# Probabilities turned one slot behind their scores in the front slots, and idle products in the first slots and at the fp8 rows

## The chip, the cores and the metric

The kernel runs on one core of a Trainium2 chip. The metric is the device time of one execution in microseconds. Five engines work side by side and meet only at semaphores: TensorE (PE in the profile, with its weight loads as PEld), VectorE (DVE), ScalarE (ACT), GpSimd (POOL) and SyncE (SP), whose queue issues the DMAs.

## What is computed

The reference is a stack of four pairs of cross-attention and feed-forward on x of 32 sequences x 64 rows x 128 columns, with a context of the same shape. The residual stream x runs through all of them:

```python
x = x + _L0_xattn_ref(_layernorm(x), ctx, mask, ...)   # 16 heads of width 64
x = x + _L0_ffn_ref(_layernorm(x), ...)                # six layers of local attention and a gated MLP
x = x + _L1_xattn_ref(_layernorm(x), ctx, ctx, ...)    # 16 heads of width 8
x = x + _L1_ffn_ref(_layernorm(x), ...)                # rows quantised to fp8, one product
x = x + _L2_xattn_ref(...); x = x + _L2_ffn_ref(...)   # experts, top 2 of 8, and a shared one
x = x + _L3_xattn_ref(...); x = x + _L3_ffn_ref(...)   # experts, top 2 of 8
```

The change lies in the small cross-attentions L1 and L2 (`n` = 0, 1 in the code), as far as they run ahead of the experts. For a tile of 128 rows (two sequences) one of them is: normalise x, project queries, keys and values, scores of 16 heads (128 x 1024 logits), subtract the maximum, exp, product with the values, divide by the sum, output projection, add to x.

## The kernel before, in words

x lies in SBUF as 16 tiles of 128 rows. `layers_*` run L0 (some 1600 us), then `merged_*` run the rest as a row of *slots* u = 0, 1, 2, ... A slot holds up to one piece of each of three *works* in flight. A work W is one small cross-attention of one tile; in the front slots, u < `LEAD` = 16, work W starts in slot W. In the program, `work` is the one that starts (u), `before` the one of the slot before (u - 1), `before2` the one before that (u - 2). From slot 16 on each slot also carries an expert; those slots are untouched. The order on each engine is written out by hand, and there is no scheduler.

What a work does, with the lines of the kernel before:

- in slot W: TensorE turns the normalised x (`turn_x`, L1676), ScalarE copies it (L1880), TensorE makes keys (L1723), values (L1732) and queries (L1739); ScalarE adds biases and copies (`front`, L1893 and L1895), VectorE spreads the keys over eight groups of heads (`keys`, L2016);
- in slot W + 1: scores (L1704) into a bank of PSUM, two of which are used: `w0` for odd W from 3 to 11, `w1` for the rest; VectorE takes maxima and subtracts them (`shift`, L1998, L2000), ScalarE makes the exp (L1901), TensorE turns the probabilities back into the same bank (eight transposes, L1750), ScalarE copies them to `probT` (L1907);
- in slot W + 2: product with the values (`attend`, L1687), VectorE divides by the sums (L2007, L2010), TensorE turns the rows (L1714), ScalarE adds a bias (L1886), TensorE makes the output product (`rows`, L1744), VectorE adds it to x (L2023) and takes statistics (L476, L478), from which GpSimd makes a scale and a shift in four small steps;
- in slot W + 3: ScalarE normalises the new x with them (`fresh_normalise`, L1912).

The output product L1744 also waits until VectorE has spread the keys of the slot's own work. The scores of a work wait until the bank's previous probabilities are copied. In slots 7 and 11 (`PRODUCT_AT`) the fp8 rows come in: VectorE quantises four tiles at the end of the slot before (L2124 to L2133, 5.2 us), TensorE turns them (L1795), ScalarE copies them (L1917), TensorE multiplies (L1803), ScalarE copies (L1978), VectorE adds (L2139). `occupy` (L1761) is a product of the identity with a weight into a bank that nobody reads (an idle product); it does no part of the computation. In slots 0 to 3 the last pieces of L0 run too (`layers_in_slot`): slot 1 has three hidden chunks of its MLP (L841, L847) and their output product (L853); VectorE's gate L1209 stands between.

Of the kernel before, what the change touches and what calls it, by code (L numbers as in the profile page):

```python
# [18 lines left out]
PAIRS = HEADS // 2  # L19
# [547 lines left out]
def layers_tensor(pe, k):  # L567
# [264 lines left out]
    def end_hidden(Q, c):  # L832
        at, n = CHUNKS[c]
        xnT = quad_buffers(k, Q).xnT
        if c:
            pe.wait_ge(k.gated, 3 * Q + c)
        else:
            pe.wait_ge(k.xn_ready, Q + 1)
            if Q < LAST:
                pe.wait_ge(k.qT_ready, FIRST + STEPS)  # L840
        pe.matmul(k.end.gates[0:n, :], k.c_w1[:, HID + at:HID + at + n], xnT[:, :], start=True,  # L841
                  stop=True).then_inc(k.gate_psum, 1)
        if c:
            pe.wait_ge(k.hid_ready, 3 * Q + c)
        elif Q == LAST:
            pe.wait_ge(k.z_fed, LAST)
        pe.matmul(k.end.lines[0:n, :], k.c_w1[:, at:at + n], xnT[:, :], start=True, stop=True).then_inc(k.line_psum, 1)  # L847

    def end_output(Q):
        pe.wait_ge(k.hid_ready, 3 * Q + 3)  # L850
        for c in range(3):
            n = CHUNKS[c][1] + (c == 2)
            mm = pe.matmul(k.end.lines, k.c_w2[0:n, c, :], quad_buffers(k, Q).hid[0:n, c, :], start=(c == 0), stop=(c == 2))  # L853
        mm.then_inc(k.out_psum, 1)

    def end_of_layers():
# [12 lines left out]
        end_hidden(LAST - 1, 2)  # L869
        end_in()  # L870

    def in_slot(u, place):

        if (u, place) == (0, "end"):
            end_output(LAST - 1)
            turn_out(1)
        if (u, place) == (1, "scores"):
            end_turn()
        if (u, place) == (1, "end"):
            for c in range(3):  # L880
                end_hidden(LAST, c)
            end_output(LAST)
        if (u, place) == (2, "end"):
            turn_out(2)
        if (u, place) == (3, "end"):
            turn_out(3)
# [4 lines left out]
    for g in range(-TILES, STEPS + 1):  # L891
        this, before, before2 = stages_of(g)
# [584 lines left out]
LEAD = 16  # L1477
END_SLOTS = 2
# [91 lines left out]
def on_w0(W):  # L1570

    return W % 2 == 1 and END_SLOTS < W < LEAD - 3
# [16 lines left out]
def merged_tensor(pe, k, layers_in_slot):  # L1589
    d = k.d  # L1590
# [78 lines left out]
    def turn_x(W, u):  # L1669
        pe.wait_ge(k.norm.normed, PHANTOM + W + TILES + 1)  # L1670
        pe.wait_ge(d.q_ready, started(u))
        pe.wait_ge(d.v_ready, started(u))
        pe.wait_ge(d.oT_ready, started(u - 2))
        if u == 0:
            pe.wait_ge(k.xn_ready, LAST)
        pe.transpose(k.pt[:, 0:P], k.normed[:, W % 2, :], k.ident[:, :]).then_inc(d.xT_psum, 1)  # L1676
# [66 lines left out]
        pe.wait_ge(d.k8_ready, started(u + 1))  # L1743
        pe.matmul(k.py[:, P:2 * P], k.s_oT[:, :], k.s_w[:, n, 3, :], start=True, stop=True).then_inc(d.y_psum, 1)  # L1744

    def turn_pairs(W, pairs):
        w = logits_bank(k, W)
        pe.wait_ge(d.exp, PHANTOM + W + 1)
        for h in pairs:
            mm = pe.transpose(w[:, h * P:(h + 1) * P],  # L1750
                              k.prob[:, W % 2, 2 * h:2 * h + 2, :].rearrange("p a m -> p (a m)"), k.ident[:, :])
        return mm

    def turn_probs(W):
        turn_pairs(W, range(PAIRS)).then_inc(d.pT_psum, 1)

    def occupy():

# [5 lines left out]
    def front_slot(u, work, before, before2):  # L1764
        if work:
            turn_x(work[2], u)
        if before:
            scores(before[2])
        layers_in_slot(u, "scores")
        if work:  # L1770
            keys(*work, u)
        if before2:
            attend(before2[2], u)
        if work:
            values(work[0], work[2], u)
            queries(work[0], work[2])
        if u in PRODUCT_AT:
            turn_quantised(PRODUCT_AT[u])
        layers_in_slot(u, "end")
        if u > END_SLOTS:  # L1780
            occupy()
        if before2:
            turn_rows(before2[2], u)
        if before:
            turn_pairs(before[2], range(PAIRS // 2))
        if before2:
            rows(before2[0], before2[2], u)
        if before:
            turn_pairs(before[2], range(PAIRS // 2, PAIRS)).then_inc(d.pT_psum, 1)

    def turn_quantised(q):
        pe.wait_ge(k.f.quantised, q + 1)
# [70 lines left out]
def merged_scalar(act, k, layers_in_slot):  # L1863
    d = k.d
# [64 lines left out]
    for u in range(SLOTS):  # L1929
        work, before, before2 = work_at(u), work_at(u - 1), work_at(u - 2)  # L1930
        job = job_at(u)
        if job:
            gelu(job, 0)
        if work:
            turned_x(work[2])
        if work_at(u - 3):
            fresh_normalise(*work_at(u - 3)[1:])
        if job:
            gelu(job, 1)
        if u in PRODUCT_AT and u >= LEAD:  # L1940
            turned_quantised(PRODUCT_AT[u])
        if job:
            gelu(job, 2)
        if before2 and u >= LEAD:
            turned_rows(before2[0], before2[2], u)
        if job:
            gelu(job, 3)
        layers_in_slot(u, "turned x")
        if work:
            front(work[0], work[2])  # L1950
        layers_in_slot(u, "front")
        if u < LEAD:
            if u in PRODUCT_AT:
                turned_quantised(PRODUCT_AT[u])
            if before:
                exp(before[0], before[2])
            if before2:
                turned_rows(before2[0], before2[2], u)
            if before:
                turned_probs(before[2])  # L1960
        if u in GATES_TURN_AT:
            e, q = GATES_TURN_AT[u]
            act.copy(k.m_gateT[0:NE[e], 512 * q:512 * q + 512], full(("gates", e, q))[0:NE[e], :]).then_inc(k.ring_read, 1)
        if u in TURN_AT:
            e, q = TURN_AT[u]
            act.copy(k.m_xT[:, q, :], full(("turn", e, q))).then_inc(k.ring_read, 1)
        if u in GATES_AT:
            quad_exp(*GATES_AT[u])
        if before and u >= LEAD:
            exp(before[0], before[2])  # L1970
        if (before and u >= LEAD) or u in GATES_AT or u == LEAD - 1:
            gelu_table(u)
        if before and u >= LEAD:
            turned_probs(before[2])
        if u in PRODUCT_AT:
            q = PRODUCT_AT[u]
            act.wait_ge(k.f.done, q)
            act.copy(k.f_prod, full(("product", q))).then_inc(k.ring_read, 1)  # L1978
        if u in RAW_AT:
            w = full(("raw", 1, RAW_AT[u]))  # L1980
            act.copy(k.m_projT[:, :], w)
            act.activation(k.m_sq[:, :], w, ACT.Square).then_inc(k.ring_read, 1)
        if u in LOGITS_AT:
            e, q = LOGITS_AT[u]
            n = 36 if e else 32
            act.copy(k.m_raw[:, 0:n], full(("logits", e, q))[:, 0:n]).then_inc(k.ring_read, 1)
        if u == SIM_AT:
            act.copy(k.m_simT[:, :], full(("sim", 1, 0))[:, 0:8]).then_inc(k.ring_read, 1)
# [491 lines left out]
```

## Time and profile before

| | us |
|---|---|
| median of 3 timed runs | 2417.6 (2416.79 to 2418.31) |
| the profiled execution, its own time | 2425.08 |
| span of its trace | 2423.3 |
| TensorE busy | 2342.5 (97%) |
| VectorE busy | 1870.4 (77%) |
| ScalarE busy | 1505.6 (62%) |
| GpSimd busy | 1216.4 (50%) |
| mean granted clock of TensorE | 0.987 |

The front slots take the stretch from 1610 to 1758 us of the trace. The engines' shares are averages over the whole program, so what the change does has to be read in that stretch alone: which wait ends last in a slot, how long a slot is, and which clock TensorE was granted there (1.00 is 2.4 GHz, 0.50 is 1.2 GHz).

### The profile page before, as it was taken

To read this page: it belongs to the slowest core of one execution; us is meant where nothing else is said; L and a number is where in the kernel's file an instruction comes from. 1 tells how busy PE (TensorE), PEld (TensorE's weight loads), DVE (VectorE), ACT (ScalarE), POOL (GpSimd) and SP (SyncE) were. 2 spreads that over 40 slices of the span, in tenths; PEclk is the share of its full clock that TensorE was granted. 3 is DMA by queue.
4 is the path that set the end of the run, shared out by engine and by line. 5 is a ranking of instruction groups with operands and counts; after the bars stand their busy time and mean duration, and the time that the engine had idled before them with its cause. 6 is when DMAs were issued, how large, how long until landed. Compare 5 with 4: busy or idle time off the path is not lost.

```text
span 2423.3 us, 61019 instructions
## 1 busy us (share of the span) xinstructions
PE 2342.5 (97%) x25478; PEld 1422.6 (59%) x25478; DVE 1870.4 (77%) x3328; ACT 1505.6 (62%) x2190; POOL 1216.4 (50%) x1028
## 2 busy tenths in 40 slices
PE   8998999999999999999999999987899999999998
PEld 6785566666666666666666666655445555455443
DVE  6989989999999999999999989957756765445222
ACT  3444666666666666666666666654477777566443
POOL 2336777777777777777777777722211121111000
PEclk9999999999999999999999999998899999999999
DMA  3000000000000000000000100002010110120110
GB/s 129 9 7 6 2 2 28 11 8 7 28 11 8 7 28 11 13 2 28 10 13 3 35 2 11 2 4 89 9 38 9 41 33 15 55 86 29 38 41 22
DMA packets 36183, 56.30 MB, mean 23 GB/s; under 512 B 6396, under 2 KB 20868, under 8 KB 35656
## 3 DMA queue, kind: packets, MB, share of 16 engines
q1 hardware_dynamic: 35912, 52.40, 6.8%
q8 instruction: 205, 3.36, 0.6%
q14 instruction: 66, 0.54, 0.1%
HBM read 51.19 MB, written 1.19 MB: 22 GB/s over the span
## 4 chain that ended last, share of the span: by engine, by line
PE 73%; DVE 19%; ACT 4%; issue 3%; POOL 1%; DVEq 0%; ACTq 0%; POOLq 0%
PE w L1621 9%; PE w L1611 9%; PE w L679 6%; PE w L660 6%; PE w L670 5%; DVE turned L1161 4%; PE w L430 4%; PE py L700 4%; PE w L724 3%; PE w L753 3%; PE w L734 2%; DVE norm L1168 2%; PE pt L783 2%; PE py L787 2%; PE w L1750 2%
## 5 line engine op out<-in xcount | busy, mean ns | idle before, releaser
L441 ACT ACTIVATE prob<-logit 128x512 f32<-128x512 f32 x224 | 137.9, 632 | 285.0 <-DVE logit L449 285.0
L1611 PE MATMUL w<-qT,m_fc 128*128 128x512 f32 x544 | 267.8, 605 | 0.4 <-ACT turned L1875 0.4
L1346 POOL TENSOR_TENSOR straight_odd<-straight_odd,turned 128x1024 f32<-128x1024 f32 x96 | 226.6, 2371 | 65.6 <-DVE turned L1161 65.6
L471 POOL TENSOR_TENSOR prob<-prob,rden 128x1024 f32<-128x1024 f32 x112 | 213.9, 1909 | 91.0 <-DVE rden L460 91.0
L1161 DVE TENSOR_TENSOR turned<-w,rot 128x512 f32<-128x512 f32 x384 | 245.5, 681 | 0.0
L1346 POOL TENSOR_TENSOR straight<-straight,turned 128x1024 f32<-128x1024 f32 x96 | 226.7, 2372 | 36.1 <-DVE turned L1161 36.1
L1340 POOL TENSOR_TENSOR straight_odd<-straight_odd,rnorms 128x1024 f32<-128x1024 f32 x96 | 180.7, 1903 | 118.2 <-DVE rnorms L1182 118.2
L1168 DVE TENSOR_REDUCE norm<-sq 128x16 f32<-128x1024 f32 x192 | 224.2, 1209 | 0.0
L490 POOL TENSOR_TENSOR fresh_roots<-fresh_means,eps 128x1 f32<-128x1 f32 x64 | 12.3, 191 | 386.1 <-DVE fresh_means L478 386.1
L1340 POOL TENSOR_TENSOR straight<-straight,rnorms 128x1024 f32<-128x1024 f32 x96 | 180.7, 1903 | 42.9 <-DVE rnorms L1182 42.9
L679 PE MATMUL w<-b_wqkv,m_proj 128*128 128x512 f32 x384 | 190.4, 618 | 1.9 <-DVE logit L449 1.9
L660 PE MATMUL w<-b_wqkv,m_proj 128*128 128x512 f32 x384 | 190.4, 618 | 0.0
L670 PE MATMUL w<-b_wqkv,m_proj 128*64 128x512 f32 x768 | 186.0, 605 | 3.3 <-DVE oT L1141 3.3
L700 PE MATMUL py<-oT,b_wo 128*128 128x256 f32 x768 | 181.5, 379 | 0.0
L2060 DVE SCALAR_TENSOR_TENSOR gate<-w,m_bcol,b_wqkv 128x512 f32<-128x512 f32 x60 | 45.0, 751 | 160.6 <-PE w L1621 160.4
L700 PEld LDWEIGHTS py<-oT,b_wo 128*128 128x128 f32 x768 | 142.2, 190 | 38.2 <-issue 23.3
L1875 ACT ACTIVATE turned<-w,m_bfc 128x512 f32<-128x512 f32 x136 | 93.4, 688 | 104.0 <-PE w L1611 102.3
L1875 ACT ACTIVATE straight_odd<-w,m_bfc 128x512 f32<-128x512 f32 x136 | 93.6, 689 | 99.9 <-PE w L1611 98.3
L1068 ACT COPY qT<-w 128x1024 f32<-128x1024 f32 x96 | 97.4, 1015 | 93.0 <-PE w L712 91.4
L457 DVE TENSOR_REDUCE den<-prob 128x8 f32<-128x512 f32 x224 | 143.5, 682 | 10.1
L1611 PEld LDWEIGHTS w<-qT,m_fc 128*128 128x128 f32 x544 | 92.1, 191 | 97.7 <-issue 88.8
L430 PEld LDWEIGHTS w<-probT,v 64*64 64x64 f32 x7168 | 115.1, 135 | 56.0 <-issue 52.3
(290 smaller groups left out, 5353.3 us busy)
## 6 DMA issues: line engine op xcount, KB each, us to landing
b_wqkv<-gates SPq DMA_DIRECT2D x64, 256.0 KB, 3.6
b_wqkv<-in_b_wqkv SPq DMA_DIRECT2D x18, 512.0 KB, 3.5
ctxT<-in_ctxT SPq DMA_DIRECT2D x64, 64.0 KB, 1.8
b_wo<-in_b_wo SPq DMA_DIRECT2D x6, 512.0 KB, 4.0
m_fc<-in_m_fc SPq DMA_DIRECT2D x1, 2304.0 KB, 8.5
m_proj<-in_m_proj SPq DMA_DIRECT2D x1, 2304.0 KB, 13.1
m_fc<-in_m_fc SPq DMA_DIRECT2D x8, 256.0 KB, 3.4
m_proj<-in_m_proj SPq DMA_DIRECT2D x8, 256.0 KB, 3.4
```

The source lines that it names most:

```text
L430: mm = pe.matmul(w[64 * c:64 * c + 64, at:at + 64], k.v2[r, s, b, 64 * h:64 * h + 64], k.probT[r, h, 64 * b:64 * b + 64], start=True, stop ...
L471: pool.tensor_tensor(flat, flat, k.rden[:, s, :, None].broadcast_to([P, HEADS, SEQ]), ALU.mult).then_inc(k.prob_ready, 1)
L660: mm = pe.matmul(k.w0[:, 512 * c:512 * c + 512], shifted_rows(k, g % TILES), k.b_wqkv[:, 512 * c:512 * c + 512], start=True, stop=True)
L670: mm = pe.matmul(k.w2[64 * p:64 * p + 64, 512 * b:512 * b + 512], k.z[:, 2 * t + b, :], k.b_wqkv[:, 2048 + 512 * p:2560 + 512 * p], start= ...
L679: mm = pe.matmul(k.w1[:, 512 * c:512 * c + 512], shifted_rows(k, g % TILES), k.b_wqkv[:, 1024 + 512 * c:1536 + 512 * c], start=True, stop= ...
L700: mm = pe.matmul(k.py[:, 0:2 * P], k.b_wo[:, h, :], k.oT[:, h, :, :].rearrange("p a n -> p (a n)"), start=(h == 0), stop=(h == PAIRS - 1))
L1161: last = dve.tensor_tensor(k.turned[:, i, :, to], heads[:, :, of], rot[:, 2 * i + 1, None, to].broadcast_to([P, HEADS, half]), ALU.mult)
L1168: dve.tensor_reduce(k.norm2[:, i, :], k.sq[:, i, :, :], AX.X, ALU.add).then_inc(norm2, 1)
L1340: pool.tensor_tensor(k.straights[s][:, i, :, :], k.straights[s][:, i, :, :], k.rnorms[:, s, i, :, None].broadcast_to([P, HEADS, HD]), ALU. ...
L1346: pool.tensor_tensor(k.straights[s][:, i, :, :], k.straights[s][:, i, :, :], k.turned[:, i, :, :], ALU.add).then_inc(added, 1)
L1611: pe.matmul(claim(("hidden", J, c)), k.m_fc[:, x, c * P:(c + 1) * P], k.m_xT[:, q, :], start=True, stop=True).then_inc(k.ring_full, 1)
L1621: mm = pe.matmul(acc, k.m_proj[:, x, c, :], k.m_hid[J % 2][:, c, :], start=(c == 0), stop=(c == 3))
```

## The change

In the front slots TensorE turns the probabilities of a work in the slot after its scores' slot: `turn_probs(before2)` instead of `turn_pairs(before)`. Where the two works use one bank (`together`: slots 2, 3, 14 and 15) it stands before the scores, elsewhere behind them. `attend` moves behind the queries. In slot 15 the last probabilities are turned at the slot's end as well, since slot 16 is as it was. On ScalarE the copy `turned_probs` moves from the slot's end to a place behind `fresh_normalise` and ahead of `front`, and the exp moves behind `turned_rows`. Idle products are added: one behind each hidden chunk in slot 1 (`layers_idle`), two before and two behind the turned fp8 rows in slots 7 and 11, and one in slot 2. VectorE's, GpSimd's and SyncE's instructions keep their order.

```diff
--- before.py
+++ after.py
@@ -869,6 +869,10 @@
         end_hidden(LAST - 1, 2)
         end_in()
 
+    def layers_idle():
+
+        pe.matmul(k.end.turn, k.ident[:, :], k.s_w[:, 0, :, :].rearrange("p a n -> p (a n)"), start=True, stop=True)
+
     def in_slot(u, place):
 
         if (u, place) == (0, "end"):
@@ -879,6 +883,7 @@
         if (u, place) == (1, "end"):
             for c in range(3):
                 end_hidden(LAST, c)
+                layers_idle()
             end_output(LAST)
         if (u, place) == (2, "end"):
             turn_out(2)
@@ -1743,16 +1748,13 @@
         pe.wait_ge(d.k8_ready, started(u + 1))
         pe.matmul(k.py[:, P:2 * P], k.s_oT[:, :], k.s_w[:, n, 3, :], start=True, stop=True).then_inc(d.y_psum, 1)
 
-    def turn_pairs(W, pairs):
+    def turn_probs(W):
         w = logits_bank(k, W)
         pe.wait_ge(d.exp, PHANTOM + W + 1)
-        for h in pairs:
+        for h in range(PAIRS):
             mm = pe.transpose(w[:, h * P:(h + 1) * P],
                               k.prob[:, W % 2, 2 * h:2 * h + 2, :].rearrange("p a m -> p (a m)"), k.ident[:, :])
-        return mm
-
-    def turn_probs(W):
-        turn_pairs(W, range(PAIRS)).then_inc(d.pT_psum, 1)
+        mm.then_inc(d.pT_psum, 1)
 
     def occupy():
 
@@ -1764,29 +1766,35 @@
     def front_slot(u, work, before, before2):
         if work:
             turn_x(work[2], u)
+        together = before and before2 and on_w0(before[2]) == on_w0(before2[2])
+        if together:
+            turn_probs(before2[2])
         if before:
             scores(before[2])
         layers_in_slot(u, "scores")
+        if before2 and not together:
+            turn_probs(before2[2])
         if work:
             keys(*work, u)
+            values(work[0], work[2], u)
+            queries(work[0], work[2])
         if before2:
             attend(before2[2], u)
-        if work:
-            values(work[0], work[2], u)
-            queries(work[0], work[2])
         if u in PRODUCT_AT:
+            occupy()
+            occupy()
             turn_quantised(PRODUCT_AT[u])
+            occupy()
+            occupy()
         layers_in_slot(u, "end")
-        if u > END_SLOTS:
+        if u >= END_SLOTS:
             occupy()
         if before2:
             turn_rows(before2[2], u)
-        if before:
-            turn_pairs(before[2], range(PAIRS // 2))
         if before2:
             rows(before2[0], before2[2], u)
-        if before:
-            turn_pairs(before[2], range(PAIRS // 2, PAIRS)).then_inc(d.pT_psum, 1)
+        if before and u == LEAD - 1:
+            turn_probs(before[2])
 
     def turn_quantised(q):
         pe.wait_ge(k.f.quantised, q + 1)
@@ -1946,17 +1954,19 @@
         if job:
             gelu(job, 3)
         layers_in_slot(u, "turned x")
+        if before2 and u < LEAD:
+            turned_probs(before2[2])
         if work:
             front(work[0], work[2])
         layers_in_slot(u, "front")
         if u < LEAD:
             if u in PRODUCT_AT:
                 turned_quantised(PRODUCT_AT[u])
-            if before:
-                exp(before[0], before[2])
             if before2:
                 turned_rows(before2[0], before2[2], u)
             if before:
+                exp(before[0], before[2])
+            if before and u == LEAD - 1:
                 turned_probs(before[2])
         if u in GATES_TURN_AT:
             e, q = GATES_TURN_AT[u]
```

TensorE, one front slot that holds nothing special (slot 5), before. The names: `normed` is the normalised tile, `straight` and `s_qT` keys and queries, `ctxT` the context, `s_v` the values, `s_rows` the divided rows, `s_oT` the turned rows.

```order
L1676 MATMUL pt<-ident,normed 128x128
L1704 MATMUL w1<-straight,s_qT 64x512 x4
L1723 MATMUL py<-ctxT,s_w 128x128
L1687 MATMUL w2<-s_v,probT 64x18 x16
L1732 MATMUL pt<-s_w,ctxT 64x64 x4
L1739 MATMUL pt<-xT,s_w 128x128
L1761 MATMUL w2<-s_w,ident 128x512
L1714 MATMUL w2<-ident,s_rows 128x128
L1750 MATMUL w1<-ident,prob 128x128 x4
L1744 MATMUL py<-s_w,s_oT 128x128
L1750 MATMUL w1<-ident,prob 128x128 x4
```

The same slot now:

```order
L1681 MATMUL pt<-ident,normed 128x128
L1709 MATMUL w1<-straight,s_qT 64x512 x4
L1755 MATMUL w0<-ident,prob 128x128 x8
L1728 MATMUL py<-ctxT,s_w 128x128
L1737 MATMUL pt<-s_w,ctxT 64x64 x4
L1744 MATMUL pt<-xT,s_w 128x128
L1692 MATMUL w2<-s_v,probT 64x18 x16
L1763 MATMUL w2<-s_w,ident 128x512
L1719 MATMUL w2<-ident,s_rows 128x128
L1749 MATMUL py<-s_w,s_oT 128x128
```

The transposes went from both sides of the output product to behind the scores, in the other bank, and belong to the work before; the attend that reads their copy went from behind the keys to behind the queries.

ScalarE, a slot of the same kind, before:

```order
L1880 COPY xT<-pt 128x128
L1912 ACTIVATE y_all<-x_all,fresh_below,fresh_roots 128x128
L1893 ACTIVATE s_qT<-pt,s_cols 128x128
L1895 COPY s_v<-pt 64x16x8 x2
L1901 ACTIVATE prob<-logit 128x1024
L1886 ACTIVATE s_oT<-w2,s_cols 128x128
L1907 COPY probT<-w1 128x1024
```

and now:

```order
L1888 COPY xT<-pt 128x128
L1920 ACTIVATE y_all<-x_all,fresh_below,fresh_roots 128x128
L1915 COPY probT<-w0 128x1024
L1901 ACTIVATE s_qT<-pt,s_cols 128x128
L1903 COPY s_v<-pt 64x16x8 x2
L1894 ACTIVATE s_oT<-w2,s_cols 128x128
L1909 ACTIVATE prob<-logit 128x1024
```

The copy of the probabilities went from the end of the row to behind the fresh normalisation, whose input is GpSimd's, and the exp to the end.

TensorE in slot 15, now, with what follows it (before, the slot reads like slot 5 before):

```order
L1681 MATMUL pt<-ident,normed 128x128
L1755 MATMUL w1<-ident,prob 128x128 x8
L1709 MATMUL w1<-straight,s_qT 64x512 x4
L1728 MATMUL py<-ctxT,s_w 128x128
L1737 MATMUL pt<-s_w,ctxT 64x64 x4
L1744 MATMUL pt<-xT,s_w 128x128
L1692 MATMUL w2<-s_v,probT 64x18 x16
L1763 MATMUL w2<-s_w,ident 128x512
L1719 MATMUL w2<-ident,s_rows 128x128
L1749 MATMUL py<-s_w,s_oT 128x128
L1755 MATMUL w1<-ident,prob 128x128 x8
L1640 MATMUL w2<-ident,y_all 128x128 x4
```

Here both rows of transposes and the scores are in bank `w1`: the transposes stand first, and a second set closes the slot.

## Rows read from the trace of the kernel before

**Rows 1.** The page, busy time of each engine, share of the span, instructions.
```profile
PE 2342.5 (97%) x25478; PEld 1422.6 (59%) x25478; DVE 1870.4 (77%) x3328; ACT 1505.6 (62%) x2190; POOL 1216.4 (50%) x1028
```

**Rows 2.** Stretches of slots 3, 4, 5+6, 7+8, 9+10, 11+12, 13, 14+15: length, busy, clock.
```profile
1640.97:1652.92 11.95, 10.97 (x76) 7.16 (x75) 6.15 (x13) 3.90 (x8) 2.24 (x7) 0.50 0.02 7
1652.92:1660.85 7.93, 5.99 (x69) 3.74 (x68) 6.17 (x13) 3.90 (x8) 2.23 (x7) 1.00 0.29 82
1660.85:1674.18 13.33, 11.74 (x135) 7.29 (x133) 10.97 (x22) 7.79 (x16) 4.46 (x14) 1.00 0.83 331
1674.18:1695.70 21.52, 15.67 (x143) 9.80 (x140) 17.19 (x36) 8.78 (x18) 5.26 (x14) 0.80 0.03 7
1695.70:1709.83 14.13, 12.55 (x134) 7.75 (x134) 10.97 (x22) 7.80 (x16) 4.46 (x14) 0.94 0.04 11
1709.83:1731.02 21.19, 14.99 (x142) 9.16 (x141) 17.19 (x36) 8.79 (x18) 5.26 (x14) 0.84 0.03 8
1731.02:1740.84 9.82, 9.76 (x68) 6.06 (x66) 5.49 (x11) 3.90 (x8) 2.23 (x7) 0.52 0.02 7
1740.84:1756.87 16.03, 12.33 (x134) 7.71 (x134) 10.97 (x22) 7.79 (x16) 4.46 (x14) 0.97 0.03 9
```

**Rows 3.** TensorE in time, slot 5: start, length, instruction.
```profile
1660.40 0.45 PE L1744 MATMUL py<-s_w,s_oT 128*128 128x128 f32 x2
...
1661.33 1.09 PE L1704 MATMUL w<-straight,s_qT 64*64 64x512 f32 x8
...
1662.77 1.11 PE L1687 MATMUL w<-s_v,probT 128*64 128x18 f32 x32
...
1664.42 1.02 PE L1761 MATMUL w<-s_w,ident 128*128 128x512 f32 x2
...
1667.06 0.46 PE L1744 MATMUL py<-s_w,s_oT 128*128 128x128 f32 x2
```

**Rows 4.** VectorE in time, slot 5: start, length, [idle before, what ended it].
```profile
1660.89 0.29 DVE L2023 TENSOR_TENSOR x_all<-x_all,py 128x128 f32<-128x128 f32 x1 [0.64 <-PE py L1744]
...
1662.48 1.23 DVE L1998 TENSOR_REDUCE top<-w 128x16 f32<-128x1024 f32 x1 [0.23 <-PE w L1704]
...
1665.43 0.29 DVE L2010 TENSOR_TENSOR s_rows<-w,rden 128x128 f32<-128x128 f32 x1
1665.64 1.28 DVE L2016 SCALAR_TENSOR_TENSOR straight<-py,s_cols,member 128x1024 f32<-128x1024 f32 x1
```

**Rows 5.** ScalarE in time, slot 5, and one row of slot 7.
```profile
1661.33 1.01 ACT L1907 COPY probT<-w 128x1024 f32<-128x1024 f32 x1 [1.07 <-PE w L1750]
...
1663.33 0.49 ACT L1912 ACTIVATE y_all<-x_all,fresh_below,fresh_roots 128x128 f32<-128x128 f32 x1 [0.82 <-POOL fresh_below L2201]
...
1677.38 0.49 ACT L1912 ACTIVATE y_all<-x_all,fresh_below,fresh_roots 128x128 f32<-128x128 f32 x1 [1.54 <-POOL fresh_below L2201]
```

**Rows 6.** TensorE in time, single rows of slots 7, 8, 13 and 14.
```profile
1679.55 0.40 PE L1795 MATMUL w<-ident,xnT 128*128 128x128 bf16 x4 [1.62 <-DVE xnT L2131]
...
1687.31 1.09 PE L1704 MATMUL w<-straight,s_qT 64*64 64x512 f32 x8
...
1731.51 1.99 PE L1704 MATMUL w<-straight,s_qT 64*64 64x512 f32 x8
...
1742.88 1.09 PE L1704 MATMUL w<-straight,s_qT 64*64 64x512 f32 x8 [1.04 <-ACT probT L1907]
```

**Rows 7.** One stretch of slot 7, columns as in rows 2.
```profile
1684.02:1687.10 3.08, 3.08 (x15) 2.66 (x16) 1.90 (x4) 0.79 (x3) 0.00 (x0) 0.51 0.00 0
```

**Rows 8.** VectorE in time, slots 7 and 8.
```profile
1683.39 0.25 DVE L2007 RECIPROCAL rden<-w 128x16 f32<-128x16 f32 x1
1683.68 0.29 DVE L2010 TENSOR_TENSOR s_rows<-w,rden 128x128 f32<-128x128 f32 x1
...
1688.50 1.36 DVE L2139 SCALAR_TENSOR_TENSOR x_all<-xs,f_scale,x_all 128x128 f32<-128x128 f32 x4 [1.49 <-ACT xs L1978]
```

**Rows 9.** TensorE in time, slot 1, the output product of the MLP.
```profile
1628.54 2.85 PE L853 MATMUL w<-v,c_w 128*128 128x512 f32 x6 [0.84 <-DVE v L1209]
```

The columns of rows 2 and 7: start:end, length, then busy time (and instructions) of PE, PEld, DVE, ACT and POOL, the granted clock of TensorE, the DMA share, GB/s.

## The prediction

> **What bounds the kernel now.** I read the engines' busy shares first: TensorE 2342.5 us of a span of 2423.3, so on the page it is the bound [rows 1]. But the change touches only the 16 front slots, about 150 us, and there the share hides the shape. Next I cut the trace at the end of each slot's output product (line 1744), which gives slot lengths and the granted clock [rows 2]: slots 5 and 6 take 13.33 us together at full clock, slots 3 and 13 take 11.95 and 9.82 at about half of it (1.2 GHz), slots 7+8 and 11+12 take 21.52 and 21.19. Then one steady slot, engine by engine, from the end of the product of slot 4 (t = 0, at 1660.40 + 0.45 = 1660.85) to the end of the next (1667.52): 6.67 us. On TensorE 1.02 us of it is an idle product [rows 3] and 0.8 us are gaps (11.74 busy of 13.33 for two slots) [rows 2]. VectorE [rows 4] adds the output at 0.04, takes the maxima at 1.63, has the scaled rows ready at 1665.72 (4.87), then spreads the keys (line 2016, 1.28 us). The product that ends the slot starts at 1667.06, 0.14 behind the end of the key spreading at 1666.92, and ends at 1667.52. So a slot ends 1.8 us after the scaled rows, call that moment S: a row ready later moves the slot's end one for one. ScalarE [rows 5] copies the turned probabilities at 1661.33, and does the fresh normalisation of an older tile at 1663.33, since that waits for GpSimd: 2.48 after t = 0, always. Today that wait holds up nobody: the copy stands ahead of it.
>
> **The change, part by part.**
>
> *Probabilities one slot later.* Per slot 8 transposes stay 8, and the exp, the copy and the output's bias are the same instructions. What moves is who waits. In the changed order ScalarE does: copy of the turned x, fresh normalisation, copy of the probabilities, biases. The copy now stands behind the wait for GpSimd. Steady slot, from rows: fresh normalisation 2.48 to 2.97, copy of 1.01 us [rows 5] overlapping its end slightly, 2.88 to 3.89, TensorE's attend at 3.95 (0.06 later, as transposes follow the exp), 1.11 us long [rows 3], to 5.06. VectorE's reciprocal and scaling after it: 5.11 to 5.68 = S (0.58 us for the two) [rows 8]. The maxima chain alone would give S at 4.7, so the attend is the later one. Slot length S + 1.8 = 7.48 against 6.67: **0.81 us longer**. TensorE fits: turned x, scores, 8 transposes, keys, values, queries take it to 3.3, where it waits 0.65 us for the copy. The exp follows the bias at once and ends about 0.1 into the next slot, before its transposes at 1.1: no cost.
>
> *Slots 3, 14 and 15*, in which the probabilities and the next scores use one bank. The transposes come first, then the scores must wait for the copy: 3.95 to 5.04. VectorE needs 3.24 us from the start of the maxima (5.09) to S (1662.48 to 1665.72) [rows 4], so S = 8.33 and the slot is 10.1 us. Today the scores there wait 1.04 us [rows 6] and the two slots 14+15 take 16.03 together. So +4.2 for both at full clock. In slot 3 TensorE also turns an output; 10.25 against 11.95: -1.7.
>
> In these slots TensorE is idle from about 1.2 to 3.95. The trace shows what such stretches bring: after the waits around 1730 the clock went to 1.2 GHz, and slot 13 ran at 0.52 [rows 2], with 1.99 us for the scores instead of 1.09 [rows 3, 6]. Estimated from the lengths of [rows 3] at up to twice: the scores take 2.0, the next three products 2, the attend 1.9, the idle product 1.7, the turned rows, bias and output 1.5: the slot ends at 12.8 instead of 10.1, and 13.5 in slot 3. That is +9.6 for slots 14+15, and +1.55 for slot 3. Both ends stay for the range.
>
> On this stands one sentence of the Trainium skill (TensorE: Matmul & The Clock Gate, Part 4: PE-mode transpose): the transpose mode doesn't count as PE-busy the same way. The trace speaks against it here: the 3.08 us from 1684.02 hold 15 TensorE instructions, 9 of them fp32 transposes, at 1.2 GHz, and right behind them the scores take 1.09 us, the length of the 2.4 GHz level [rows 6, 7]. By the rule the slots 3, 14 and 15, which put eight transposes ahead of the gap, would all run low, the upper end of what follows; by the row only part of them.
>
> *The end of slot 15.* The last probabilities are turned after slot 15's output; their copy precedes the copy that the first gate logits wait for. Exp to 0.1, transposes 0.15 to 1.2, copies to 3.2, where today they are half done before the output. From row differences: +1.1, or +1.7 at the low clock.
>
> *Slots 7 and 11 (fp8 rows).* VectorE's quantising keeps S where it is, 9.8 us after the slot's start (1683.68 + 0.29 against the start at 1674.18) [rows 2, 8]. Four more idle products of 0.86 us and the moved attend lie in TensorE's queue: attend to 5.7 (beside the quantising GpSimd is slower: fresh normalisation at 1677.38, 3.2 after the start [rows 5], so the copy ends at 4.6), two idle products to 7.4, the turned fp8 rows, which could have gone at 5.4 [rows 6], to 7.8, the copy to 8.4, three idle products to 11.0. The turned rows then leave at 11.0 instead of 9.9, and the slot ends at 12.3 against 11.9: these products are not free, +0.35 each. What they buy is the clock behind them: slots 8 and 12, with VectorE's product added at 1.2 instead of 2.4 after the start (1688.50 less 1686.08 [rows 8]; no copy of probabilities ahead of it), reach S = 6.3 and end at 8.1, against 9.6 and 9.3 today. So 7+8: 20.35 against 21.52, -1.2; 11+12: 20.35 against 21.19, -0.8. If the clock falls at the attend's 1.4 us wait, each idle product costs 1.7 us and the slot 4 us more: kept for the range.
>
> *Slot 1, idle products between the hidden chunks.* TensorE's one wait of note there is the 0.84 us before the output product [rows 9]; between the chunks it hardly waits. So two of the three products push, at 0.8 and 0.65 us each, and the third lies in the wait: +1.3 on the output product. Slot 2 gives it back, since the exp and half of the transposes no longer stand before its output: +0.1 at its end, and a full clock into slot 3 instead of 0.50.
>
> *The rest.* Slot 4 waits for VectorE's add before its scores, then the copy: 8.25 against 7.93, +0.3. Slots 5+6: +1.6. Slots 9+10: 14.96 against 14.13, +0.8. Slot 13: 7.48 against 9.82, -2.3, if the clock stays up.
>
> **Sum**, full clock everywhere: 0.1 - 1.7 + 0.3 + 1.6 - 1.2 + 0.8 - 0.8 - 2.3 + 4.2 + 1.1 = **+2.1**. With the low clock in slots 3, 14 and 15: 0.1 + 1.55 + 0.3 + 1.6 - 1.2 + 0.8 - 0.8 - 2.3 + 9.6 + 1.7 = **+11.3**. Idle stretches of 1.3 to 2.3 us on both sides of short work were enough to drop it at slots 3, 8, 12 and 13 today, and here the stretch is 2.75; it drops somewhere in the slot and not at its start, so I take two thirds of the difference: +8.2. The sums are made within the profiled execution (span 2423.3, its own time 2425.1); the median of the timed runs is 2417.6, and a difference inside 150 us is carried over unchanged: 2425.8.
>
> **Rivals.**
> A, the forecast: the copy behind GpSimd's wait sets the slots, low clock in much of slots 3, 14, 15. 2425.8, from 2422.5 to 2429. Chance 0.45.
> B: the same wait, but the clock holds: 2419.7. For it: slots 14 and 15 today hold 0.97 through waits of 1.04, 0.3 and 0.5 us. Against: one gap of 2.75. Chance 0.22.
> C, the other side: the fresh normalisation gets its input early and the copy is not late. This decides at 2.15 after the output's end, when the transposes finish; GpSimd's answer would have to come 0.3 us sooner. Then attend ends at 4.3, S stays at 4.7, steady slots are 6.5, slots 14 and 15 8.4, slot 3 8.6, slot 13 6.5. Sum: -3.4 - 0.5 - 0.4 - 1.6 - 1.2 - 1.3 - 3.3 + 0.8 + 1.1 = -9.8: 2407.8. Against: 2.48 in every slot read. Chance 0.12.
> D: the clock falls too in a slot with fp8 rows or behind it (+4): 2430 to 2434. Chance 0.13.
> E: the change doesn't do what it says: slots stay at VectorE's pace, the idle products only shift the low stretches about; 2416 to 2420. Chance 0.08.
>
> **How the numbers follow.** 2425.8 is A's. The range from 2413.5 to 2434 takes in A, B, D, E and half the way to C; it leaves out C and a little of D. A measurement here tells 0.2% (4.8 us) from no change: faster is C, 0.12; same is B, E and the lowest part of A, 0.33; slower is the rest of A and D, 0.55.
>
> **What would show it.** Right: in the changed profile the copy of the probabilities starts directly behind the fresh normalisation in slots 4 to 13; TensorE waits for it ahead of the attend, about 0.65 us; steady slots of 7.4 to 7.5; scores of slots 14 and 15 waiting over 2 us, then at 1.2 GHz; slot 13 at full clock. Wrong: steady slots of 6.5 to 6.7, or an attend that waits for nothing (C); scores of 1.09 us behind the long gap (B); a fp8 slot over 14 us (D).

## The result, and the profile after

| | before | changed |
|---|---|---|
| median, us | 2417.19 (2416.20 to 2418.31, 4 runs) | 2438.41 (2435.10 to 2439.75, 4 runs) |
| ratio | | 1.0083, 95% interval 1.0070 to 1.0096 (the two medians alone: 1.0088) |
| span of the trace | 2423.3 | 2435.7 |

The change makes the kernel 21.2 us slower. The direction was forecast, the size was not: 2425.8 with a range to 2434. The two traces differ by only 12.4 us, and the first experiment is about that.

The changed kernel, the same stretches as in [rows 2] (slots 3, 4, 5+6, 7+8, 9+10, 11+12, 13, 14+15; start:end, length, busy time and instructions of PE, PEld, DVE, ACT, POOL, granted clock, DMA share, GB/s):

```profile
1639.77:1651.13 11.36, 8.10 (x76) 4.68 (x74) 6.24 (x13) 3.51 (x9) 2.23 (x7) 0.85 0.03 7
1651.13:1661.04 9.91, 7.47 (x67) 5.13 (x66) 6.26 (x13) 4.08 (x9) 2.22 (x7) 0.83 0.30 94
1661.04:1675.95 14.91, 11.85 (x133) 7.60 (x132) 11.00 (x22) 7.51 (x17) 4.43 (x14) 1.00 0.70 277
1675.95:1697.64 21.69, 17.64 (x149) 10.33 (x148) 16.97 (x36) 8.59 (x19) 5.26 (x14) 0.92 0.02 7
1697.64:1712.55 14.91, 11.85 (x134) 7.56 (x132) 11.00 (x22) 7.43 (x16) 4.44 (x14) 1.00 0.04 12
1712.55:1734.04 21.49, 17.45 (x149) 10.04 (x148) 16.97 (x36) 8.58 (x19) 5.27 (x14) 0.92 0.02 7
1734.04:1741.50 7.46, 5.98 (x68) 3.77 (x66) 5.50 (x11) 3.68 (x9) 2.22 (x7) 1.00 0.03 9
1741.50:1767.65 26.15, 20.55 (x132) 12.17 (x131) 11.15 (x22) 7.50 (x17) 4.43 (x14) 0.59 0.02 6
```

Slots 3 to 15 take 127.9 us against 115.9 in the first trace of before. Slots 5, 6, 9, 10 and 13 take 7.45 or 7.46 each at full clock. The row of slots 14+15 holds the largest loss, and it is the one with the lowest clock.

One steady slot, TensorE in time (start, length, [idle before, what ended it]), against [rows 3]:

```profile
1661.08 1.09 PE L1709 MATMUL w<-straight,s_qT 64*64 64x512 f32 x8
1662.10 1.09 PE L1755 MATMUL w<-ident,prob 128*128 128x128 f32 x8
...
1664.95 1.11 PE L1692 MATMUL w<-s_v,probT 128*64 128x18 f32 x32 [0.73 <-ACT probT L1915]
...
1668.04 0.46 PE L1749 MATMUL py<-s_w,s_oT 128*128 128x128 f32 x2 [0.81 <-DVE straight L2026]
```

and ScalarE in the same slot, against [rows 5]:

```profile
1661.18 0.27 ACT L1888 COPY xT<-pt 128x128 f32<-128x128 f32 x1
1663.51 0.49 ACT L1920 ACTIVATE y_all<-x_all,fresh_below,fresh_roots 128x128 f32<-128x128 f32 x1 [2.06 <-POOL fresh_below L2211]
1663.91 0.99 ACT L1915 COPY probT<-w 128x1024 f32<-128x1024 f32 x1
1666.19 0.37 ACT L1901 ACTIVATE s_qT<-pt,s_cols 128x128 f32<-128x128 f32 x1 [1.29 <-PE w L1692]
```

The transposes are done at 1663.19. ScalarE stands at the fresh normalisation until 1663.51, since it waits for GpSimd, and only then copies. TensorE waits 0.73 us for the copy, and the slot's output product waits 0.81 us for VectorE's spread keys, which stand behind the rows that the attend made late.

Slot 14, where both works use one bank:

```profile
1741.64 1.09 PE L1755 MATMUL w<-ident,prob 128*128 128x128 f32 x8
1745.50 1.40 PE L1709 MATMUL w<-straight,s_qT 64*64 64x512 f32 x8 [2.77 <-ACT probT L1915]
...
1748.91 1.90 PE L1692 MATMUL w<-s_v,probT 128*64 128x18 f32 x32
1750.74 2.07 PE L1763 MATMUL w<-s_w,ident 128*128 128x512 f32 x2
```

TensorE sits idle for 2.77 us; within the scores behind it the clock falls to 1.2 GHz, the attend takes 1.90 us instead of 1.11 and the idle product 2.07 instead of 1.13. It stays there through slot 15, which takes 13.36 us, and through what follows, up to the first expert product. The first two rows are the changed kernel's, behind slot 15's end at 1767.65; the third is the kernel before's first expert product, 3.00 us behind the end of its slot 15 at 1756.87:

```profile
1767.81 1.97 PE L1755 MATMUL w<-ident,prob 128*128 128x128 f32 x8 [0.15 <-ACT prob L1909]
...
1773.16 2.05 PE L1616 MATMUL w<-qT,m_fc 128*128 128x512 f32 x2
```

```profile
1759.87 1.10 PE L1611 MATMUL w<-qT,m_fc 128*128 128x512 f32 x2
```

### The profile page after: what moved, and what is told of

It is laid out like the page before. It is cut to its first block, busy times and chain, and to the rows that moved or that the text cites. A ratio compares the mean times of both kernels' runs of the same rounds, so it can differ in the third digit from the quotient of the medians.

```text
span 2435.7 us, 61067 instructions
## 1 busy us (share of the span) xinstructions
PE 2354.5 (97%) x25502; PEld 1428.3 (59%) x25502; DVE 1869.9 (77%) x3328; ACT 1501.9 (62%) x2190; POOL 1215.1 (50%) x1028
## 3 DMA queue, kind: packets, MB, share of 16 engines
HBM read 51.19 MB, written 1.19 MB: 22 GB/s over the span
## 4 chain that ended last, share of the span: by engine, by line
PE 72%; DVE 19%; ACT 4%; issue 3%; POOL 1%; DVEq 0%; ACTq 0%; POOLq 0%
PE w L1626 9%; PE w L1616 9%; PE w L679 6%; PE w L660 6%; PE w L670 5%; DVE turned L1166 4%; PE w L430 4%; PE py L700 4%; PE w L724 3%; PE w L753 3%; PE w L734 2%; DVE norm L1173 2%; PE pt L783 2%; PE py L787 2%; PE w L712 2%
## 6 DMA issues: line engine op xcount, KB each, us to landing
m_proj<-in_m_proj SPq DMA_DIRECT2D x1, 2304.0 KB, 13.1
```

## The experiments

Line numbers are those of the changed kernel, a few off in each variant. The expectations name some runs by short labels: e1 is the kernel before measured again, e3 the idle products alone, e4 the copy ahead of the fresh normalisation, e7 each order where it is shorter. The runs were made at different times, so differences between two variants of a few us carry the uncertainty of both intervals.

### The kernel before, measured again

No edit.

> The kernel before, unchanged, looked at a second time. Its profiled execution took 7.9 us more than the median of its timed ones, that of the changed kernel about as much as its own median, so the two traces show 12.4 us of the 21.2. Theory Z (executions of the kernel before differ in which front slots run at 1.2 GHz, and the profiled one was a bad one): slots 3 to 15 (from the end of the output product of slot 2 to that of slot 15), 115.9 us in the first trace, come out at 105 to 110, with slot 3 or slot 13 at full clock. Rival (the difference lies in what surrounds the span, or in the layers before slot 0): 115 to 117 again. Ratio 1.000 either way.

> A third look at the kernel before. Theory Z: slots 3, 7, 8, 11 and 12 as in both looks, slots 9 and 13 once more at 6.7 or once more long; the sum of slots 3 to 15 at 111 where no further slot fell to 1.2 GHz, 114 to 116 where one did.

Measured: the second time 2418.19 us (ratio 0.9998, 0.9989 to 1.0008), the span of its trace 2416.3; the third time one run, 2420.5, span 2418.7. Slots 3 to 15 took 111.0 and 114.4 us, against 115.9 in the first trace. Second trace: slots 3, 9+10, 13 and 14+15; then slot 13 of the third:

```profile
1638.28:1650.11 11.83, 10.85 (x77) 7.04 (x76) 6.14 (x13) 3.89 (x8) 2.24 (x7) 0.51 0.02 7
...
1692.52:1705.84 13.32, 11.74 (x135) 7.29 (x133) 10.95 (x22) 7.79 (x16) 4.45 (x14) 1.00 0.04 12
...
1727.02:1733.69 6.67, 5.88 (x69) 3.65 (x67) 5.47 (x11) 3.89 (x8) 2.22 (x7) 1.00 0.03 10
1733.69:1749.30 15.61, 11.87 (x134) 7.35 (x133) 10.96 (x22) 7.79 (x16) 4.44 (x14) 1.00 0.03 9
```

```profile
1726.52:1736.29 9.77, 9.72 (x67) 6.04 (x66) 5.48 (x11) 3.88 (x8) 2.22 (x7) 0.52 0.02 7
```

Slot 3 ran low in all three traces (11.95, 11.83, 11.59), slot 13 in two of three (9.82, 6.67, 9.77); slot 9 took 7.46 in one and 6.67 in two. So executions of one kernel differ by which front slots fall to 1.2 GHz. The trace that the prediction was made from was the longest of the three: its execution took 2425.1 us, that of the second 2418.1. Of these 7.0 us 4.9 lie in slots 3 to 15, and 1.7 before slot 0's first transpose (1610.41 against 1608.71). Theory Z holds in kind: slot 13 was back at full clock, but the sum came out at 111.0 where it had said 105 to 110. Against the second trace the account of the change closes: slots 3 to 15 +16.9, from there to the first expert product +2.4 (5.51 against 3.07), up to slot 3 +1.5, behind it -1.4: 19.4, the difference of the spans 2435.7 and 2416.3.

### The changed kernel, measured again

No edit.

> A second look at the changed kernel. Theory X: slots 5, 6, 9, 10 and 13 at 7.45 whatever the clock did elsewhere; slots 14 and 15 at 12.8 to 13.4 each, since the gap of 2.7 us is there in each execution; the sum of slots 3 to 15 at 126 to 131.

Measured: one run, 2439.57. Slots 5, 6, 9, 10 and 13: 7.46 each again. Slots 14 and 15: 12.96 and 13.38. Slots 3 to 15: 128.1 us. As expected. The two traces of this kernel agree to 0.2 us where the three of the kernel before spread over 4.9, but two traces don't make it steady: two variants below, with the same instructions in slot 3, took 13.10 us there instead of 11.3 to 11.4.

### One half of the change at a time

Probabilities moved, without the idle products:

```diff
             for c in range(3):
                 end_hidden(LAST, c)
-                layers_idle()
...
         if u in PRODUCT_AT:
-            occupy()
-            occupy()
             turn_quantised(PRODUCT_AT[u])
-            occupy()
-            occupy()
         layers_in_slot(u, "end")
-        if u >= END_SLOTS:
+        if u > END_SLOTS:
             occupy()
```

> The changed kernel without any of the twelve added idle products (slots 1, 2, 7 and 11). Theory X (the move of the probabilities costs, by the copy behind the fresh normalisation and the low clock behind the long gaps of slots 3, 14 and 15): 2433 to 2440, near the changed kernel, steady slots still 7.46 us, slots 14+15 again 24 to 26 us. Theory Y (the idle products cost): 2418 to 2424.

Measured: 2436.01 us, ratio 1.0070 (1.0053 to 1.0087), inside theory X's range; slots 14+15, at 26.76, lie a little above its 24 to 26. Its slots 3 and 14+15:

```profile
1637.54:1650.64 13.10, 9.84 (x76) 6.24 (x74) 6.23 (x13) 3.82 (x9) 2.24 (x7) 0.69 0.02 6
1739.46:1766.22 26.76, 21.14 (x132) 12.29 (x131) 11.14 (x22) 7.52 (x17) 4.44 (x14) 0.54 0.02 6
```

The idle products alone, on the kernel before: the same lines added there.

```diff
             for c in range(3):
                 end_hidden(LAST, c)
+                layers_idle()
...
         if u in PRODUCT_AT:
+            occupy()
+            occupy()
             turn_quantised(PRODUCT_AT[u])
+            occupy()
+            occupy()
         layers_in_slot(u, "end")
-        if u > END_SLOTS:
+        if u >= END_SLOTS:
             occupy()
```

> The kernel before with the idle products alone, the probabilities turned as before. Theory X: within 3 us of 2417.2 (slot 1 +1.3, fp8 slots +0.3 to +1 each, less low clock behind them -1 to -2 each). Theory Y: 2425 to 2435.

Measured: 2416.46 us, ratio 0.9995 (0.9984 to 1.0006). In its trace slot 3 and slots 7+8:

```profile
1638.31:1646.11 7.80, 6.29 (x76) 4.07 (x75) 6.14 (x13) 3.89 (x8) 2.24 (x7) 1.00 0.04 11
1667.35:1688.11 20.76, 16.63 (x150) 9.54 (x148) 17.15 (x36) 8.86 (x18) 5.34 (x14) 0.98 0.03 8
```

Against the second trace of before, slot 3 lost its low clock (11.8 to 7.8 us) and slots 7+8 gained 0.4, while slots 9 and 13 ran partly low (7.91 and 7.32). That trace had 108.05 us for slots 3 to 15; over the timed runs no difference is left that stands clear of the interval. The idle products alone cost nothing that can be measured, and the move alone costs 17.5 us (2436.01 against 2418.48, the kernel before timed beside it), most of the 21.2. Theory X stands and Y falls in both runs.

### The copy ahead of the fresh normalisation

```diff
         if work:
             turned_x(work[2])
+        if before2 and u < LEAD:
+            turned_probs(before2[2])
         if work_at(u - 3):
             fresh_normalise(*work_at(u - 3)[1:])
...
         layers_in_slot(u, "turned x")
-        if before2 and u < LEAD:
-            turned_probs(before2[2])
```

> The changed kernel with ScalarE's copy of the probabilities ahead of the fresh normalisation, so that it doesn't stand behind GpSimd's wait; nothing else moves. Theory X: the attend starts 3.3 instead of 3.95 us after the previous output, steady slots of 6.8 instead of 7.46; slots 3, 14 and 15 wait 1.1 instead of 2.7 us for the copy and last 8.5 at full clock: slots 14+15 near 17 instead of 26; in all 12 to 16 us less than the changed kernel, 2423 to 2426. Rival (the spread keys or the turned rows set the slots whatever the copy does): steady slots stay at 7.4 or more and it ends within 4 us of 2438.

Measured: 2416.13 us, ratio 0.9989 (0.9979 to 0.9999): 22.3 us less than the changed kernel, more than the 12 to 16 expected. ScalarE and TensorE in a steady slot:

```profile
1666.53 1.02 ACT L1915 COPY probT<-w 128x1024 f32<-128x1024 f32 x1 [1.78 <-PE w L1755]
1667.44 0.49 ACT L1920 ACTIVATE y_all<-x_all,fresh_below,fresh_roots 128x128 f32<-128x128 f32 x1
```

```profile
1667.60 1.11 PE L1692 MATMUL w<-s_v,probT 128*64 128x18 f32 x32
```

and its stretches of slots 5+6, 7+8 and 14+15:

```profile
1657.55:1671.14 13.59, 11.84 (x133) 7.55 (x132) 11.00 (x22) 7.55 (x17) 4.44 (x14) 1.00 0.78 308
1671.14:1690.31 19.17, 16.23 (x149) 9.54 (x148) 16.96 (x36) 8.80 (x19) 5.27 (x14) 1.00 0.03 8
...
1729.86:1746.91 17.05, 12.68 (x133) 7.59 (x132) 10.95 (x22) 7.84 (x17) 4.44 (x14) 1.00 0.03 9
```

The attend waits for nothing, starts 3.26 us after the previous output (1664.34) and the slots take 6.8. The rival, that the keys set the slots whatever the copy does, falls. In slots 3, 14 and 15 a wait for the copy is left, 1.19 us instead of 2.7, and the clock is full in every slot but slot 4. Moving one ScalarE instruction by one place takes the whole loss back. Against the second trace of before this one has 108.06 us for slots 3 to 15 instead of 111.02: it gives away 1.4 in slots 14+15 (17.05 against 15.61) and 2.1 in slot 4, and gains 3.1 in slot 3 and 2.0 in each pair with fp8 rows (19.17 against 21.17 in 7+8).

### The wait kept, the clock held

Three idle products behind the turned probabilities in slots 3, 14 and 15, two ahead of the scores in slot 4:

```diff
         if together:
             turn_probs(before2[2])
+            if u > END_SLOTS:
+                for i in range(3):
+                    occupy()
+        if u == END_SLOTS + 2:
+            occupy()
+            occupy()
```

> The changed kernel with idle products laid into the gaps alone: three behind the turned probabilities in slots 3, 14 and 15, where TensorE waited 2.7 us for the copy, and two ahead of the scores of slot 4. The copy still stands behind the fresh normalisation, so the wait stays and only the clock is treated. Theory X splits the price of a one-bank slot in a wait and a low clock: slots 14+15 go from 26.15 to 20.2 (10.1 each, against 15.6 in the kernel before), slot 3 to 10.3, slot 4 to 8.3, and the whole to 2425 to 2429. Rival (the scores' wait alone makes them long, the low clock costs nothing since TensorE isn't last there): slots 14+15 stay at 25 to 26, time within 3 us of 2438.

Measured: 2425.37 us, ratio 1.0033 (1.0021 to 1.0046). Slots 14+15, and TensorE in slot 14:

```profile
1738.39:1758.76 20.37, 17.84 (x146) 9.69 (x144) 10.95 (x22) 7.61 (x17) 4.43 (x14) 1.00 0.03 8
```

```profile
1738.54 1.09 PE L1755 MATMUL w<-ident,prob 128*128 128x128 f32 x8
1739.46 2.74 PE L1763 MATMUL w<-s_w,ident 128*128 128x512 f32 x6
1742.40 1.09 PE L1709 MATMUL w<-straight,s_qT 64*64 64x512 f32 x8 [0.20 <-ACT probT L1921]
```

The scores start no earlier, 4.0 us after the previous output as in the changed kernel, but nothing behind them is slow: 20.37 against 26.15, slot 3 10.19 against 11.36, slot 4 8.51 against 9.91. The medians differ by 13.0 us, so that much of the 21.2 was the low clock behind these gaps, with the uncertainty of two medians; the two traces show 10.1 of it in the places that were treated (5.8 in slots 14+15, 1.2 and 1.4 in slots 3 and 4, 1.8 up to the first expert product). The other 8 are the waits themselves and what low clock is left: slots 7 and 11 took 14.16 and 15.42 here.

### What the idle products are worth where nothing waits for GpSimd

The kernel with the copy ahead of the fresh normalisation, less the twelve added idle products (that edit and the one of the first half above, together).

> The kernel of e4 (copy ahead of the fresh normalisation) without the twelve added idle products. Tells what they are worth where nothing waits behind GpSimd. If they hold the clock behind the fp8 rows and in slots 2 and 3: 3 to 7 us above e4, that is 2420 to 2423, with slots 8 and 12 at 8.3 to 9.3 instead of 7.6 and a low clock in slot 3. If they do nothing: within 2 us of 2416.

Measured: 2421.68 us, ratio 1.0017 (1.0005 to 1.0030): 5.6 us above the same kernel with them. In its trace slot 3 is back at 13.1 us (clock 0.50), slots 8 and 12 at 9.10 and 8.95. In this order they pay; two of the ten timed runs without them took 2429 and 2431.

### The fp8 slots

```diff
         if u in PRODUCT_AT:
-            occupy()
-            occupy()
             turn_quantised(PRODUCT_AT[u])
```

> The changed kernel without the two idle products ahead of the turned fp8 rows in slots 7 and 11; the two behind them stay. In its trace these two ran at 1.2 GHz (3.39 and 3.21 us for the pair) behind a wait of 1.46 us for the copy, and the slots took 14.1 and 13.9. Theory X: the fp8 rows are turned right behind the attend, at 1.2 GHz too or not, and both slots come to 11.9 to 12.6: 3 to 4 us less than the changed kernel, unless slots 8 and 12 then run low and give 1 to 1.7 us each back: 2433 to 2437. Rival (something else in the slot sets its length, such as the turned rows): 13.5 to 14.1 again.

Measured: 2437.42 us, ratio 1.0090 (1.0074 to 1.0107), no difference from the changed kernel. First the changed kernel in slot 7, then this one in slots 7 and 11:

```profile
1680.59 1.34 PE L1692 MATMUL w<-s_v,probT 128*64 128x18 f32 x32 [1.46 <-ACT probT L1915]
1681.85 3.39 PE L1763 MATMUL w<-s_w,ident 128*128 128x512 f32 x4
1685.07 0.39 PE L1803 MATMUL w<-ident,xnT 128*128 128x128 bf16 x4
1686.14 2.84 PE L1763 MATMUL w<-s_w,ident 128*128 128x512 f32 x6 [0.68 <-ACT xnT L1925]
```

```profile
1682.23 4.54 PE L1763 MATMUL w<-s_w,ident 128*128 128x512 f32 x6 [1.27 <-ACT xnT L1923]
...
1717.69 5.49 PE L1763 MATMUL w<-s_w,ident 128*128 128x512 f32 x6 [1.27 <-ACT xnT L1923]
```

Without the leading pair slot 7 takes 12.94 instead of 14.09, but slot 11 takes 14.00 as before, because the three behind the turned rows then run at 1.2 GHz themselves (5.49 us). Behind the attend's wait of 1.45 us the clock fell in both kernels, and some idle products took the slow time, whichever they were; with the copy first, where the attend doesn't wait, both slots ran at full clock and took 11.57. The expected 3 to 4 us are a miss.

### Each order where it is shorter

Works 4 to 11 turn late, with the copy ahead of the fresh normalisation, the others as before the change. The edit is shown against the kernel before:

```diff
+LATE = range(4, 12)
...
+        if before2 and before2[2] in LATE:
+            turn_probs(before2[2])
         if work:
             keys(*work, u)
-        if before2:
+        if before2 and before2[2] not in LATE:
             attend(before2[2], u)
         if work:
             values(work[0], work[2], u)
             queries(work[0], work[2])
+        if before2 and before2[2] in LATE:
+            attend(before2[2], u)
...
-        if before:
+        early = before and before[2] not in LATE
+        if early:
             turn_pairs(before[2], range(PAIRS // 2))
         if before2:
             rows(before2[0], before2[2], u)
-        if before:
+        if early:
             turn_pairs(before[2], range(PAIRS // 2, PAIRS)).then_inc(d.pT_psum, 1)
...
+        if before2 and u < LEAD and before2[2] in LATE:
+            turned_probs(before2[2])
         if work_at(u - 3):
             fresh_normalise(*work_at(u - 3)[1:])
```

The idle products of the change are added too, and ScalarE's exp follows the same choice.

> Each order where the traces have it shorter: works 4 to 11 turn their probabilities one slot later with the copy ahead of the fresh normalisation, works 0 to 3 and 12 to 14 turn them as before, all idle products of the change kept. Theory X: slots 3, 4, 14, 15 as in e3 (7.8, 7.9, 7.8, 7.8), slots 5 to 13 as in e4 (6.7, 6.8, 11.6, 7.6, 6.8, 6.8, 11.6, 7.6, 7.0): 105 for slots 3 to 15 against 111 in e1, time 2410 to 2412, below both kernels. Rival (the two orders disturb each other at slots 5 and 13, or the timed executions fall to the low clock anyway): 2415 to 2418.

> The kernel of e7 without the added idle products. If the later turn itself helps around the fp8 rows (slots 8 and 12, VectorE's add no longer behind a copy): 2414 to 2416. If the gain of e7 is the idle products': 2417 to 2420.

Measured: with the idle products 2413.33 us (12 runs), ratio 0.9982 (0.9973 to 0.9991); without, 2415.61, ratio 0.9990 (0.9981 to 0.9999). The first is below both kernels: 4.9 us below the kernel before, timed beside it, and 25 below the changed one. The second falls in the branch where the later turn itself helps, but only just: its interval ends at 0.9999, and its trace has 111.3 us for slots 3 to 15, no less than the second trace of before. Slots 3, 7+8, 13 and 14+15 of the first:

```profile
1637.53:1645.34 7.81, 6.31 (x77) 4.08 (x75) 6.14 (x13) 3.89 (x8) 2.23 (x7) 1.00 0.04 10
...
1666.76:1685.93 19.17, 16.23 (x149) 9.55 (x148) 16.96 (x36) 8.79 (x19) 5.27 (x14) 1.00 0.03 8
...
1718.75:1726.07 7.32, 6.34 (x72) 4.29 (x72) 5.50 (x11) 3.89 (x8) 2.22 (x7) 1.00 0.03 9
1726.07:1741.68 15.61, 11.87 (x134) 7.35 (x133) 10.96 (x22) 7.78 (x16) 4.43 (x14) 1.00 0.03 9
```

Slots 3 to 15 take 104.15 us there, all at full clock. The timed runs spread from 2406.9 to 2417.2 and the traced one took 2407.2 at a mean granted clock of 0.997, where the longest ran at 0.993. So other executions do lose clock somewhere; where, no trace of them shows. The expected 2410 to 2412 was missed by 1.3 us.

## Why the prediction was right or wrong

**Right: the mechanism and its place.** The copy directly behind the fresh normalisation, the attend waiting 0.73 us (0.65 forecast), steady slots of 7.46 (7.48), the output product tied to the spread keys: all were as forecast. The scores waited 2.77 us in slot 14 and 1.89 in slot 15, where the slow transposes fill part of the gap. The full-clock length of 10.1 us for a one-bank slot was measured with the gap filled: 10.19 and 10.18. Moving the copy took the loss away (2416.13 us). Slot 1's push and slot 2's return held too: slot 2 ended 30.58 us after slot 0's first transpose, against 30.56 in the first trace of before (29.57 in the second). Rival C (attend not late) needed GpSimd's answer sooner; ScalarE waited 2.06 us for it. D's sign, a fp8 slot over 14 us, was there too (14.09 in slot 7), though the time lies above D's 2430 to 2434.

**Wrong: the size, 8.2 forecast and 21.2 measured.** Of the 13.0 us that are missing, 8.8 lie in the carrying over from the traced execution to the median (12.4 us between the two traced executions, 21.2 between the medians), and 4.2 in the sum itself. The steps that failed:

1. *The base.* "A difference inside 150 us is carried over unchanged" to the median. The slots were taken from an execution that took 7.9 us more than the median of 2417.19. The prediction had both times before it (2425.1 and 2417.6) and gave no reason why their difference should not lie in the slots. In slots 3 to 15 it was 4.9 us longer than the second trace, 4.4 of them in slots 9, 13 and 14, which ran partly or wholly low in it and at full clock in the second. The gain of 2.3 us in slot 13 was a gain against a low stretch that isn't there in every run; against the second trace slot 13 is 0.8 longer, slots 9+10 are 1.6 longer and not 0.8, slots 14+15 start from 15.61. This is the largest of the failed steps: the base makes 7.9 of the 8.8 us, and the other 0.9 is the changed kernel's traced execution, 2437.52 against its median of 2438.41.
2. *The low clock in slots 14 and 15*, taken at two thirds. Slot 14 was at 0.68 and 12.79 us, slot 15 at 0.50 all through and 13.36, above the 12.8 named as the upper end. 26.15 us, where the forecast's mixture had 23.8 and its upper end 25.6. The stretch behind, 5.51 us to the first expert product, was 2.5 more than in the first trace of before, against 1.1 to 1.7. The changed kernel's slots 14 and 15:

```profile
1741.50:1754.29 12.79, 9.53 (x67) 5.74 (x66) 5.58 (x11) 3.75 (x9) 2.22 (x7) 0.68 0.02 6
1754.29:1767.65 13.36, 11.02 (x66) 6.44 (x65) 5.57 (x11) 3.75 (x9) 2.22 (x7) 0.50 0.02 5
```

The reading that the two thirds rested on, idle stretches of 1.3 to 2.3 us at slots 3, 8, 12 and 13, doesn't fit slot 3: the idle stretches of slot 2 were 1.09, 0.79 and 1.20 us.

3. *The fp8 slots*, 12.3 forecast, 14.1 and 13.9 measured. The chance that the clock falls at the attend's wait was named and kept for the range only; in the changed kernel the pair of idle products took 3.39 and 3.21 us instead of 1.7. The pairs 7+8 and 11+12 changed by +0.2 and +0.3 us instead of -1.2 and -0.8, although slots 8 and 12 were better than forecast, 7.60 against 8.1.
4. *Slot 4*, 8.25 forecast, 9.91 measured. The changed kernel, TensorE in slot 4:

```profile
1652.87 1.09 PE L1709 MATMUL w<-straight,s_qT 64*64 64x512 f32 x8 [1.63 <-DVE x_all L1221]
1653.89 1.92 PE L1755 MATMUL w<-ident,prob 128*128 128x128 f32 x8
```

The wait for VectorE's add was in the forecast, but behind it the transposes ran at 1.2 GHz, 1.92 us instead of 1.09. With two idle products ahead of the scores the slot took 8.51.

Slot 3 went the other way, 11.36 where the low-clock estimate was 13.5, the clock being back within the slot. That too differs between executions of the same instructions. The scores of slot 3, first in the changed kernel, then in the run without the leading idle products, which has the same instructions up to slot 7:

```profile
1643.78 1.98 PE L1709 MATMUL w<-straight,s_qT 64*64 64x512 f32 x8 [2.68 <-ACT probT L1915]
```

```profile
1640.60 1.09 PE L1709 MATMUL w<-straight,s_qT 64*64 64x512 f32 x8 [2.69 <-ACT probT L1913]
```

In the first the clock was low at once and back by the attend (1.11 us), and the slot took 11.36. In the second the scores still ran at 2.4 GHz, the attend at 1.2 GHz (1.90 us), and the slot took 13.10. So scores of 1.09 us behind the long gap, the prediction's sign for B, don't tell that the clock held. Why the clock came back in slot 3 of one and not in slot 14 of either, behind gaps of 2.68 to 2.78 us, stays open.

The Trainium skill (TensorE: Matmul & The Clock Gate, Part 4: PE-mode transpose) says that a transpose doesn't count as PE-busy the same way; by that rule slots 3, 14 and 15 would all run low. Slots 14 and 15 did, slot 3 only in part. With the copy first, the same eight transposes stood ahead of the scores, the gap behind them was 1.19 instead of 2.7 us, and all three slots ran at 1.00; so the transposes alone don't bring the low clock here, and no run here isolates them.

## What to carry to other kernels

Before moving work to a later slot, write down what it will stand behind on its new engine's queue: an in-order engine that waits for a third one passes that wait to everything behind it, and one copy one place too low cost 22 us here. Price an idle gap on TensorE twice, as itself and as the low clock behind it, which was the larger part here (13 of 21 us by the medians). Don't count on idle products in advance: the twelve were worth 5.6 us in one order and nothing measurable in the kernel before, and two that ran behind a wait, at 1.2 GHz, took 3.39 us themselves. And take the base of a sum of clock-sensitive terms from several traces: a gain against a low stretch of one execution may be no gain at all.

## What the runs showed of the hardware that was not expected

The same program on the same data gave 111.0, 114.4 and 115.9 us for slots 3 to 15 in three traces, mostly by slot 13 running at 1.2 GHz or not (9.8 against 6.67 us). In the changed kernel a gap of 2.77 us in slot 14 was followed by 1.2 GHz from within the scores behind it to the end of slot 15. The twelve idle products changed nothing in the timed median of the kernel before (0.9995), though in the traced run slot 3 fell from 11.8 to 7.8 us.
